# Half rows of the adjacency matrix loaded with a cast instead of copied first, and the first support product run beside the turning of h

## The chip, the cores and the metric

The kernel runs on one core of a Trainium2 chip. The core has a matrix engine (TensorE, PE in the profile, with its weight loads shown apart as PEld), a vector engine (VectorE, DVE), an activation engine (ScalarE, ACT), a general engine (GpSimd, POOL) and a queue engine that does nothing but issue transfers (SyncE, SP). Each works through its own instructions in order, and they wait for each other on counters called semaphores. Transfers run on 16 DMA engines that all queues share. Transfers of this kernel that change the data type are all issued from POOL, the others from SP or ACT.

The metric is device time in microseconds of one execution; lower is better.

## The reference, cut to what matters

Four graph layers run over N = 2708 nodes (padded to 2816 = 22 blocks of 128) with 256 features and a sparse 0/1 adjacency matrix `adj`. Each layer is `x = x + layer(relu(layernorm(x)), adj)`. Layer 0 is graph attention with 4 heads. Layer 1 is the one that the change is about:

```
node_adj_norm = adj with a zero diagonal
node_support  = node_adj_norm @ h                      # "support"
edge_output   = gru_cell(node_support, h, edge weights)
per head: hW = h @ W;  e = leaky_relu((node_adj_norm @ hW) @ a)
          att = softmax(where(node_adj_norm > 0, e, -9e15), axis=1);  out = (att * node_adj_norm) @ hW
node_output   = gru_cell(mean of the 3 heads, h, node weights)
result        = diag * edge_output + diag * node_output
```

The softmax needs, for each row and head, the largest `e` among the row's neighbours. Layer 2 is a neighbour mean with a linear map, layer 3 a distance-weighted sum that the kernel skips at run time when a check over all of `adj` finds nothing to add.

## The kernel before

The transposed adjacency matrix is kept in SBUF as fp8 (`AT`, 22 rows of blocks), loaded by POOL with a cast (lines 666 and 686). The instruction order of each engine is written out by hand; nothing is reordered later. The stages, in order of time:

- **Layer 0** (about 93 to 394 us). For 8 units (2 halves of the columns by 4 heads) and 22 row blocks, ACT makes a threshold (line 811), DVE two masks (lines 1130, 1136), and PE multiplies them with moving tiles 65 columns wide (line 1619), 44 weight loads and matmuls per step. Rings of 6 thresholds and 12 masks lie between the engines. Beside this, POOL loads the second half of `AT` (line 686) and then, in 22 transfers (line 689), copies `adj` from fp32 in HBM to `AH_D`, a bf16 copy in HBM; each waits for four more masks (`masks_built`). SP zeroes the diagonal of that copy.
- **Turning of h** (about 402 to 427 us). Per block t: ACT normalises (line 770), POOL casts the high fp16 part (697), DVE makes the low part (1224), PE transposes (1636), ACT or DVE evicts `HTS`, and PE multiplies it with a narrow matrix (1647).
- **Scores** (to about 471 us). PE multiplies `AT` with a 10 column matrix (line 1654, 484 matmuls), DVE works the scores out in steps, and they are written out and read back spread over all partitions (`EB`). In DVE's gaps PE runs the first support product, `support(0, c)`, cut in pieces (line 1665). `support(s, c)` covers blocks 2s and 2s+1 of the result and half c of the features: 44 matmuls, 256 columns wide, into PSUM bank c.
- **Edge steps** (about 471 to 708 us), t = 0 to 21. In a step PE runs one support product ahead, the head products (1677, 1679) and the GRU's products (1710, 1717). DVE takes its share of 88 "row maxima" (`row_max`, line 1316): each reads one half row block of `adj`, 128 x 1408 in bf16 (`AROW`, two buffers), against the scores of one head. Row L of the buffers serves heads 0 and 1, so 2 maxima per load. `rows_before(t)` says how many maxima are done when step t begins: 0, 5, 9, 14, 18, 22, 27, ... DVE's order in a step is: first maximum, `gru_blend` of the step before, the middle maxima, `support_low`, `products_low`, the last maximum, `gru_new`. POOL's part is `delta(t)` (line 703), which waits for ACT's tanh after `gru_new(t)` and is waited for by `gru_blend(t)`, and `apply` (708, 709). SP loads the half rows from `AH_D` (`load_row`, line 487); row L waits until both maxima of row L-2 are done, since it takes their buffer.
- **Attention** (about 710 to 1050 us). 9 units of 22 steps on PE (lines 1760, 1761), with the 44 maxima of the third head spread over the first 104 steps on DVE.
- Then the node GRU with layer 2's linear part, layer 2's sum and the output.

Of the kernel before, what the change touches and what calls it, by code (L numbers as in the profile page):

```python
# [18 lines left out]
def gnn_stack_kernel(nc, t_in, out):  # L19
# [60 lines left out]
    with ExitStack() as ctx:  # L80
# [78 lines left out]
        ZB = a0.take(NT, dt=BF16, size=2)  # L159
# [9 lines left out]
        assert NREAL <= (P - 1) * NT  # L169
# [96 lines left out]
        NOTI = sb("NOTI", [P, P])  # L266
# [17 lines left out]
        AH_D = nc.dram_tensor("adj_rows_half", [NT, P, N], BF16, kind="Internal").ap()  # L284
# [71 lines left out]

        def loads_before(t):

            return max(2, -(-rows_before(t) // 2))
# [52 lines left out]
        def _(sp):  # L412
# [49 lines left out]
            def load_halves(to, k, name):  # L462
                sp.dma_start(to, WS_D[k]).then_inc(sem(name), 16)

            sp.wait_ge(sem("rows_h"), 16 * NT)
            sp.dma_start(AH_D.rearrange("t p n -> (t p n)")[0:(P - 1) * NT * (N + 1)]
                         .rearrange("(a b c) -> a b c", b=NT, c=N + 1)[:, :, 0:1],
                         ZB[0:P - 1, :].unsqueeze(2), allow_slow_non_contiguous=True).then_inc(sem("rows_z"), 16)
            sp.wait_ge(sem("rows_z"), 16)
# [13 lines left out]
            def load_row(L):  # L483
                t, c = half_of(L)
                if L >= 2:
                    sp.wait_ge(sem("rmax"), maxima_after(L - 2))
                sp.dma_start(AROW[:, L % 2, :], AH_D[t, :, c * QUARTER:(c + 1) * QUARTER]
                             ).then_inc(sem(f"arow{L % 2}"), 16)

# [9 lines left out]
            for L in range(2):  # L499
                load_row(L)  # L500
# [37 lines left out]
            for t in range(NT):  # L538
                if t + 2 < NT:
                    load_h(t + 2, HR, 0)  # L540
                for L in range(loads_before(t + 1) if t else 2, loads_before(t + 2)):
                    load_row(L)
# [14 lines left out]
            for L in range(2 * NT, 2 * NT + 2):  # L557
                load_row(L)
# [12 lines left out]
            for m in range(len(units1) * NT):  # L571
                n, j = divmod(m, NT)
                h, g = units1[n]
                if m in row_at and row_at[m] + 2 < 4 * NT:
                    load_row(row_at[m] + 2)
# [68 lines left out]
        def _(pool):  # L644
# [10 lines left out]
            link(pool.memset(ZB, 0.0))  # L655
# [31 lines left out]
            for t in range(NT):  # L687
                pool.wait_ge(sem("masks_built"), 68 + 4 * t)
                pool.dma_start(AH_D[t], t_in["adj"][t * P:(t + 1) * P, :]).then_inc(sem("rows_h"), 16)

# [20 lines left out]
            for t in range(NT + 1):  # L711
                if t < NT:
                    delta(t, 0, HR, GT)
# [1239 lines left out]
```

## Time and profile before

| | us |
|---|---|
| median of 3 runs | 1334.71 (1331.9 to 1335.75) |
| profiled execution | 1334.99 |
| its span in the profile | 1332.9 |
| PE busy | 1140.3 |
| DVE busy | 937.4 |
| ACT busy | 785.0 |
| POOL busy | 216.7 |

The profile is of one execution. Its page gives busy time by engine, the chain of work that ended last, groups of instructions by line and the transfers. "issue" as a releaser is time in which an engine waited for nothing that the profile shows. PEclk is the clock granted to PE, as a share of 2.4 GHz: 1.00 is 2.4 GHz and 0.50 is 1.2 GHz. Busy shares are averages over stages with different limits, so what follows reads each stage by itself.

### The profile page before, as it was taken

What the parts mean: (1) busy time and instruction counts of PE and PEld (TensorE: products, weight loads), DVE (VectorE), ACT (ScalarE), POOL (GpSimd) and SP (SyncE); (2) the same over time, 40 slices, a digit from 0 to 9 for tenths busy, and PEclk for the clock granted to TensorE, in tenths of its full rate; (3) what the DMA queues carried; (4) which work ended last, traced back from release to release, by engine and by line L of the source; (5) the groups of instructions that cost most, each with busy time, mean ns of one, the idle gap of its engine ahead of it and who ended that gap; (6) DMA issues with size and microseconds to landing.
All of it is one profiled execution on the core that took longest, in us unless ns stands there. A gap on an engine that the chain in (4) does not pass through costs nothing.

```text
span 1332.9 us, 35106 instructions
## 1 busy us (share of the span) xinstructions
PE 1140.3 (86%) x15054; PEld 938.5 (70%) x15054; DVE 937.4 (70%) x2037; ACT 785.0 (59%) x1001; POOL 216.7 (16%) x296
## 2 busy tenths in 40 slices
PE   5529897987886989899978999999999997778997
PEld 4429887887885767666656888888888654446886
DVE  5786677767896289999995998769995365553541
ACT  3479988777735123332226999989989465653000
POOL 5631010000003012222222000001220141220000
PEclk9759999999995789999999999999999998899999
DMA  9936565556307343434336345417852010020532
GB/s 216 180 51 67 62 95 115 98 111 128 63 4 267 94 128 100 126 104 129 104 114 210 106 147 180 135 59 286 281 193 104 5 30 16 16 95 1 180 125 86
DMA packets 83731, 153.68 MB, mean 115 GB/s; under 512 B 9537, under 2 KB 60337, under 8 KB 82609
## 3 DMA queue, kind: packets, MB, share of 16 engines
q1 hardware_dynamic: 74993, 127.05, 30.8%
q0 software_dynamic: 7392, 23.79, 12.9%
q8 instruction: 120, 1.97, 0.6%
q10 hardware_dynamic: 1184, 0.53, 0.1%
q14 instruction: 42, 0.34, 0.1%
HBM read 171.26 MB, written 35.60 MB: 155 GB/s over the span
## 4 chain that ended last, share of the span: by engine, by line
PE 56%; DVE 23%; issue 8%; ACT 6%; DMA 3%; POOL 3%; ACTq 0%; SPq 0%; DVEq 0%; POOLq 0%
PE PS L1619 18%; PE PS L1760 10%; PE PS L1761 10%; DVE scratch L1316 9%; PE PS L1814 8%; PE PS L1710 3%; POOL arena L703 2%; PE PS L1801 2%; DVE arena L1298 2%; DVE arena L1090 2%; PE PS L1717 1%; PE PS L1587 1%; DMA arena<-e_rows 1%; DVE arena L1342 1%; PE PS L1654 1%
## 5 line engine op out<-in xcount | busy, mean ns | idle before, releaser
L1760 PE MATMUL PS<-arena 128*128 128x257 f16 x1452 | 325.5, 272 | 7.6 <-ACT arena L897 4.4
L1619 PE MATMUL PS<-arena 128*128 128x65 f16 x7744 | 259.1, 196 | 80.8 <-issue 41.3
L1761 PE MATMUL PS<-arena 128*128 128x257 f16 x1452 | 325.5, 274 | 0.0
L1619 PEld LDWEIGHTS PS<-arena 128*128 128x128 fp8e4 x7744 | 256.4, 99 | 83.4 <-issue 81.6
L811 ACT ACTIVATE arena<-arena 128x1408 fp8e4<-128x1408 f32 x176 | 242.5, 1456 | 51.4 <-DVE arena L1130 51.1
L1316 DVE CUSTOM_DVE_ANT_0 scratch<-arena 128x1408 bf16<-128x1408 bf16 x132 | 223.2, 1691 | 23.7 <-DMA arena<-e_rows 11.1
L897 ACT ACTIVATE arena<-arena 128x896 int16<-128x896 uint8 (+1 forms) x198 | 187.3, 973 | 22.8 <-DVE arena L1371 14.7
L1760 PEld LDWEIGHTS PS<-arena 128*128 128x128 bf16 x1452 | 142.7, 98 | 32.6 <-issue 8.6
L1761 PEld LDWEIGHTS PS<-arena 128*128 128x128 bf16 x1452 | 139.9, 96 | 21.5
L1130 DVE TENSOR_TENSOR arena<-arena,AT 128x352 int32<-128x352 int32 x176 | 91.3, 519 | 83.4 <-PE PS L1619 63.3
L888 ACT ACTIVATE arena<-arena,E1B 128x896 uint8<-128x896 f32 (+1 forms) x131 | 139.3, 1064 | 2.0 <-DMA arena<-m_rows 2.0
L876 ACT ACTIVATE arena<-arena 128x256 f32<-128x256 f32 x44 | 18.3, 417 | 186.1 <-DVE arena L1342 186.1
L1710 PE MATMUL PS<-arena 128*128 128x512 f16 x528 | 122.3, 382 | 0.4 <-ACT PS L860 0.4
L1665 PE MATMUL PS<-AT,arena 128*128 128x256 fp8e4 x968 | 111.5, 275 | 0.0
L703 POOL TENSOR_TENSOR arena<-arena 128x256 f32<-128x256 f32 x44 | 47.4, 1076 | 377.8 <-ACT arena L876 377.8
L1814 PE MATMUL PS<-arena,AT 128*128 128x256 f16 x968 | 106.2, 273 | 0.8 <-DVE X L1466 0.8
L1665 PEld LDWEIGHTS PS<-AT,arena 128*128 128x128 f16 x968 | 95.6, 99 | 12.1
L1814 PEld LDWEIGHTS PS<-arena,AT 128*128 128x128 fp8e4 x968 | 94.6, 98 | 12.5 <-DVE X L1466 1.1
L1371 DVE TENSOR_TENSOR arena<-arena,AT 128x224 int32<-128x224 int32 (+1 forms) x198 | 80.1, 432 | 19.2 <-ACT arena L888 19.0
L1710 PEld LDWEIGHTS PS<-arena 128*128 128x128 f16 x528 | 51.8, 98 | 56.8 <-issue 2.7
L1136 DVE TENSOR_TENSOR arena<-arena,AT 128x352 int32<-128x352 int32 x176 | 90.8, 516 | 0.0
L1423 DVE SCALAR_TENSOR_TENSOR scratch<-arena 128x1408 fp8e4<-128x1408 f32 x44 | 73.2, 1664 | 0.8 <-DMA arena<-in_adj 0.8
(189 smaller groups left out, 1333.3 us busy)
## 6 DMA issues: line engine op xcount, KB each, us to landing
arena<-adj_rows_half SPq DMA_DIRECT2D x88, 352.0 KB, 3.1
arena<-in_adj SPq DMA_DIRECT2D x44, 704.0 KB, 5.3
adj_rows_half<-in_adj POOLq DMA_DIRECT2D x22, 704.0 KB, 8.3
hw_saved<-arena SPq DMA_DIRECT2D x22, 387.0 KB, 4.3
AT<-in_adjT POOLq DMA_DIRECT2D x44, 176.0 KB, 8.0
arena<-hw_saved SPq DMA_DIRECT2D x9, 774.0 KB, 5.8
arena<-el_rows SPq DMA_DIRECT2D x8, 704.0 KB, 11.5
arena<-h_saved SPq DMA_DIRECT2D x44, 128.0 KB, 2.1
```

Of the source, the lines that this page charges most:

```text
L811: act.activation(THR[:, m % NTHR, :], ELB[:, n % 2, :], ACT.Sigmoid, bias=ERB[:, j, h:h + 1], scale=SHARP, saturate=False).then_inc(sem("t ...
L888: act.activation(Y[:, m % NRING, 0:nb * P], MB[n % 2][:, 0:nb * P], ACT.Relu, bias=E1B[:, j * H1 + h:j * H1 + h + 1], saturate=False).then ...
L897: act.activation(PWb[:, m % NRING, 0:nb * P], Y[:, m % NRING, 0:nb * P], ACT.Copy, scale=256.0).then_inc(sem("p_ready"), 1)
L1130: dve.tensor_tensor(mask_words(m, 0), THRi[:, m % NTHR, :], adj_words(m), ALU.bitwise_and).then_inc(sem("m_plus"), 1)
L1136: dve.tensor_tensor(mask_words(m, 1), mask_words(m, 0), adj_words(m), ALU.bitwise_xor).then_inc(sem("masks_built"), 1)
L1316: dve.tensor_tensor_reduce(junk, AROW[:, L % 2, :], eb[:, c * QUARTER:(c + 1) * QUARTER], 1.0, 0.0, ALU.mult, ALU.max, M2[:, c, h * NT + t ...
L1619: ins = pe.matmul(PS[:, first_bank(n) + i, (2 * r + q) * C0:(2 * r + q + 1) * C0], MASK[:, (m + j) % NMASK, q, k * P:(k + 1) * P], MOV[:, ...
L1665: ins = pe.matmul(PS[:, c, 0:D], HHL[:, j, a, c * P:(c + 1) * P], AT[:, j, i0 * P:i1 * P], start=(j == 0 and a == 0), stop=(j == NT - 1 an ...
L1710: ins = pe.matmul(PS[:, bank, :], half(c, a), w[:, c, b, 0:2 * D], start=False, stop=(w is wih and c == DC - 1 and a == 1), skip_group_che ...
L1760: pe.matmul(PS[:, k, 0:D + 1], weights, w[:, 0:D + 1], start=(j == 0), stop=False)
L1761: ins = pe.matmul(PS[:, k, 0:D + 1], weights, w[:, D + 2:2 * D + 3], start=False, stop=(j == NT - 1))
L1814: ins = pe.matmul(o, AT[:, j, t * P:(t + 1) * P], YHL[:, j, a, :], start=(j == 0 and a == 0), stop=(j == NT - 1 and a == 1))
```

## The change

Three things are changed.

1. The bf16 copy of `adj` in HBM goes, with its 22 transfers, the zeroing of its diagonal and the waits of SP for both. `load_row` moves from SP's queue to POOL's and reads `adj` itself in fp32, casting to bf16 on the way. DVE zeroes the diagonal block in SBUF ahead of the first maximum that uses it (heads 0 and 2).
2. In POOL's loop over the edge steps, loads stand at three places: ahead of `delta(t)`, behind it, and behind `apply(t - 1)`.
3. PE runs `support(0, c)` one block at a time beside the turning of h, and `support(1, c)` in the gaps of the scores where `support(0, c)` was. Steps 0 and 1 then have no support product. ACT's and DVE's evictions of the first product move forward with it.

```diff
+            def load_row(L):
+                t, c = half_of(L)
+                if L >= 2:
+                    pool.wait_ge(sem("rmax"), maxima_after(L - 2))
+                pool.dma_start(AROW[:, L % 2, :], t_in["adj"][t * P:(t + 1) * P, c * QUARTER:(c + 1) * QUARTER]
+                               ).then_inc(sem(f"arow{L % 2}"), 16)
+            load_row(0)
+            load_row(1)
+            fetched = 2
...
             for t in range(NT + 1):
+                while t < NT and 2 * fetched < rows_before(t + 1):
+                    load_row(fetched)
+                    fetched += 1
                 if t < NT:
                     delta(t, 0, HR, GT)
+                while fetched < 2 * NT + 2 and maxima_after(fetched - 2) <= min(rows_before(t + 1) + 1, rows_before(t + 2)):
+                    load_row(fetched)
+                    fetched += 1
                 if t >= 1:
                     apply(t - 1, 0, HR)
+                while fetched < 2 * NT + 2 and maxima_after(fetched - 2) <= min(rows_before(t + 1) + 2, rows_before(t + 2)):
+                    load_row(fetched)
+                    fetched += 1
             pool.wait_ge(sem("hw_mm"), NT)
             for m in range(len(units1) * NT):
+                if m in row_at and row_at[m] + 2 < 4 * NT:
+                    load_row(row_at[m] + 2)
...
-                pool.dma_start(AH_D[t], t_in["adj"][t * P:(t + 1) * P, :]).then_inc(sem("rows_h"), 16)
...
+                if h != 1 and c == diagonal_half(t):
+                    at = t * P - c * QUARTER
+                    block = AROW[:, L % 2, at:at + P].bitcast(mybir.dt.int32)
+                    link(dve.tensor_tensor(block, block, NOTI[:].bitcast(mybir.dt.int32), ALU.bitwise_and))
                 dve.tensor_tensor_reduce(junk, AROW[:, L % 2, :], ...
...
             for t in range(NT):
                 if t + 1 < NT:
                     l1_transposes(t + 1)
...
+                support(0, 0, t, t + 1)
+                support(0, 1, t, t + 1)
...
-            support(0, 0, 0, 11)
+            support(1, 0, 0, 11)
...
-                if s + 1 < len(SUP):
+                if 2 <= s + 1 < len(SUP):
                     support(s + 1, c)
```

How this stands on POOL's queue in the first edge steps. Before (L703 is `delta`, L708 and L709 are `apply`):

```order
43 L703 TENSOR_TENSOR arena<-arena 128x256 [waits n,hr0]
44 L703 TENSOR_TENSOR arena<-arena 128x256 [waits n,hr1]
45 L708 TENSOR_SCALAR arena<-arena,DN 128x256 [waits blend]
46 L709 TENSOR_TENSOR X<-X,arena 128x256 [waits pool_chain]
47 L703 TENSOR_TENSOR arena<-arena 128x256 [waits n,hr2]
```

And after, from `delta(0)` to `delta(3)` (L673 is `load_row`, L684 `delta`, L689 and L690 `apply`):

```order
43 L684 TENSOR_TENSOR arena<-arena 128x256 [waits n,hr0]
44 L673 DMA arena<-in_adj 128x1408 [waits rmax] x2
45 L684 TENSOR_TENSOR arena<-arena 128x256 [waits n,hr1]
46 L673 DMA arena<-in_adj 128x1408 [waits rmax] x2
47 L689 TENSOR_SCALAR arena<-arena,DN 128x256 [waits blend]
48 L690 TENSOR_TENSOR X<-X,arena 128x256 [waits pool_chain]
49 L684 TENSOR_TENSOR arena<-arena 128x256 [waits n,hr2]
50 L673 DMA arena<-in_adj 128x1408 [waits rmax] x2
51 L689 TENSOR_SCALAR arena<-arena,DN 128x256 [waits blend]
52 L690 TENSOR_TENSOR X<-X,arena 128x256 [waits pool_chain]
53 L673 DMA arena<-in_adj 128x1408 [waits rmax]
54 L684 TENSOR_TENSOR arena<-arena 128x256 [waits n,hr3]
```

The loads that stood on SP's queue now stand behind `delta`, in pairs or singly; the two of row 44 are L = 3 and 4, those of row 46 are L = 5 and 6, those of row 50 are L = 7 and 8, and row 53 is L = 9.

On PE at the beginning of the turning of h, before (L1636 transposes, L1647 is the narrow product):

```order
390 L1636 MATMUL PS<-identh,arena 128x128 [waits lo1]
391 L1636 MATMUL PS<-identh,arena 128x128 x3
392 L1647 MATMUL PS<-U1S,arena 128x3 [waits hts_dve]
393 L1647 MATMUL PS<-U1S,arena 128x3 x5
394 L1636 MATMUL PS<-identh,arena 128x128 [waits hts_dve,lo1]
```

After (L1632 transposes, L1656 is the narrow product, L1643 is `support`):

```order
390 L1632 MATMUL PS<-identh,arena 128x128 [waits lo1,diag0]
391 L1632 MATMUL PS<-identh,arena 128x128 x3
392 L1656 MATMUL PS<-U1S,arena 128x3 [waits hts_dve]
393 L1656 MATMUL PS<-U1S,arena 128x3 x5
394 L1643 MATMUL PS<-AT,arena 128x256 x4
395 L1632 MATMUL PS<-identh,arena 128x128 [waits hts_dve,lo1]
```

Four matmuls 256 columns wide are added per block, 88 in all, between the narrow product of one block and the transposes of the next but one.

## Rows read from the trace of the kernel before

**Rows 1.** The page: busy time by engine, and the chain that ended last.
```profile
PE 1140.3 (86%) x15054; PEld 938.5 (70%) x15054; DVE 937.4 (70%) x2037; ACT 785.0 (59%) x1001; POOL 216.7 (16%) x296
...
PE 56%; DVE 23%; issue 8%; ACT 6%; DMA 3%; POOL 3%; ACTq 0%; SPq 0%; DVEq 0%; POOLq 0%
```

**Rows 2.** Stretches, whole core: length, busy (instructions) by engine, clock, DMA share, GB/s.
```profile
95.00:190.00 95.00, 86.02 (x2566) 85.31 (x2564) 67.62 (x146) 87.04 (x65) 10.77 (x21) 0.95 0.57 62
190.00:355.00 165.00, 132.91 (x3961) 131.08 (x3958) 117.28 (x266) 128.79 (x95) 12.12 (x23) 0.97 0.60 115
355.00:394.00 39.00, 38.29 (x1193) 38.16 (x1192) 33.51 (x82) 19.72 (x17) 0.00 (x0) 1.00 0.11 5
```

**Rows 3.** Waits, 190:355: waiter, releaser, us, times, longest.
```profile
PE PS L1619 <- issue: 30.9, 16, 3.6
```

**Rows 4.** Chain of waits, 186:356: start us, us, what.
```profile
by line: PE PS L1619 80.3%; issue 19.8%
...
229.17 3.58 issue
232.75 5.70 PE PS L1619 x128
```

**Rows 5.** The page's DMA issues: KB written each, median us to landing.
```profile
arena<-adj_rows_half SPq DMA_DIRECT2D x88, 352.0 KB, 3.1
arena<-in_adj SPq DMA_DIRECT2D x44, 704.0 KB, 5.3
```

**Rows 6.** Line 686, casting load of adjT: us from issue to landing.
```profile
DMA to landing us min/median/max: 4.1/4.4/8.7
```

**Rows 7.** Line 689, casting copy of adj: us from issue to landing.
```profile
DMA to landing us min/median/max: 6.3/8.3/12.5
```

**Rows 8.** Line 487, half-row load of before: us from issue to landing.
```profile
DMA to landing us min/median/max: 2.8/3.1/9.0
```

**Rows 9.** Timeline, DVE, 524.5:537.5: start us, us, instruction, [idle before].
```profile
524.92 1.62 DVE L1316 CUSTOM_DVE_ANT_0 scratch<-arena 128x1408 bf16<-128x1408 bf16 x1
...
527.16 0.43 DVE L1349 SCALAR_TENSOR_TENSOR arena<-arena 128x256 f32<-128x256 f32 x1 [0.61 <-POOL arena L703]
...
528.04 2.14 DVE L1316 CUSTOM_DVE_ANT_0 scratch<-arena 128x1408 bf16<-128x1408 bf16 x1
...
530.37 1.63 DVE L1316 CUSTOM_DVE_ANT_0 scratch<-arena 128x1408 bf16<-128x1408 bf16 x1 [0.17 <-DVE M L1316]
```

**Rows 10.** Timeline, POOL, same stretch.
```profile
525.59 1.53 POOL L703 TENSOR_TENSOR arena<-arena 128x256 f32<-128x256 f32 x1 [7.80 <-ACT arena L876]
```

**Rows 11.** Line 703, POOL's difference, both layers.
```profile
L703 POOL TENSOR_TENSOR arena<-arena x44: 724/728/1697, 480.7 to 1191.3; 128x256 f32<-128x256 f32 x44
```

**Rows 12.** Lines 1371 and 1211, DVE's masking of int32 words.
```profile
L1371 DVE TENSOR_TENSOR arena<-arena,AT x198: 371/389/1821, 711.6 to 1032.2; 128x224 int32<-128x224 int32 x132, 128x256 int32<-128x256 int32 x66
...
L1211 DVE TENSOR_TENSOR AT<-AT,arena x1: 184/184/184, 389.3 to 389.3; 128x32 int32<-128x32 int32 x1
```

**Rows 13.** Timeline, PE, 405:458.
```profile
406.15 1.01 PE L1636 MATMUL PS<-identh,arena 128*128 128x128 f16 x8 [12.63 <-DVE arena L1224]
...
429.06 6.56 PE L1654 MATMUL PS<-arena,AT 128*128 128x10 f16 x240 [1.67 <-DVEq L1244]
...
444.37 4.49 PE L1665 MATMUL PS<-AT,arena 128*128 128x256 fp8e4 x22
...
449.45 2.57 PE L1665 MATMUL PS<-AT,arena 128*128 128x256 fp8e4 x22
```

**Rows 14.** Stretches, as rows 2.
```profile
402.00:427.00 25.00, 15.97 (x214) 13.04 (x214) 16.29 (x47) 15.74 (x31) 10.86 (x23) 0.50 0.77 251
...
470.00:700.00 230.00, 208.18 (x1513) 147.62 (x1512) 211.12 (x354) 66.75 (x152) 56.10 (x55) 0.98 0.39 112
```

**Rows 15.** Timeline, DVE, line 1316 in 729:850, first and last of 36.
```profile
729.83 1.62 DVE L1316 CUSTOM_DVE_ANT_0 scratch<-arena 128x1408 bf16<-128x1408 bf16 x1 [5.28 <-issue]
...
849.75 1.62 DVE L1316 CUSTOM_DVE_ANT_0 scratch<-arena 128x1408 bf16<-128x1408 bf16 x1
```

More of the change, by code:

```diff
@@ L540, in _ @@
                     load_h(t + 2, HR, 0)
-                for L in range(loads_before(t + 1) if t else 2, loads_before(t + 2)):
-                    load_row(L)
                 if t == NT - 2:
@@ L556, in _ @@
                         load_products(0, c)
-            for L in range(2 * NT, 2 * NT + 2):
-                load_row(L)
             for i in range(2):
@@ L847, in support_high @@
                 act.activation(NSH[:, s % 2, c, 0, :], PS[:, c, 0:D], ACT.Copy).then_inc(sem("ns_hi"), 1)
+            for c in range(DC):
+                support_high(0, c)
+            act.wait_ge(sem("fr_arg"), 1)
+            act.activation(FR, FR, ACT.Exp).then_inc(sem("fr"), 1)
             def products_high(t):
@@ L908, in _ @@
             gate_bias_n(1, 0, BIAS)
-            for c in range(DC):
-                support_high(0, c)
             act.wait_ge(sem("frw"), 1)
@@ L1245, in _, with support_low @@
             bias_sum(BIAS, BRB, "be", "bias_e")
+            def support_low(s, c):
+                dve.wait_ge(sem("ns_hi"), DC * s + c + 1)
+                dve.tensor_tensor(NSH[:, s % 2, c, 1, :], PS[:, c, 0:D], NSH[:, s % 2, c, 0, :],
+                                  ALU.subtract).then_inc(sem("ns_lo"), 1)
+            for c in range(DC):
+                support_low(0, c)
             dve.wait_ge(sem("dn"), 16)
@@ L1372, in mask @@
                                   ).then_inc(sem("y_masked"), 1)
-            for c in range(DC):
-                support_low(0, c)
             for t in range(NT + 1):
@@ L1668, in support @@
                     ins.then_inc(sem("ns"), 1)
+            l1_transposes(0)
+            pe.wait_ge(sem("diag0"), DIAG0)
+            for t in range(NT):
+                if t + 1 < NT:
+                    l1_transposes(t + 1)
+                pe.wait_ge(sem("hts_dve" if t % 2 == 0 else "hts_act"), t // 2 + 1)
+                for c in range(DC):
+                    for a, b in TERMS:
+                        ins = pe.matmul(PS[:, 5, t * H1:(t + 1) * H1], HTS[:, t, (DC * a + c) * P:(DC * a + c + 1) * P],
+                                        U1S[:, c, b, 0:H1], start=(c == 0 and a + b == 0), stop=(c == DC - 1 and a == 1))
+                ins.then_inc(sem("hu_mm"), 1)
+                support(0, 0, t, t + 1)
+                support(0, 1, t, t + 1)
+            pe.wait_ge(sem("up"), 1)
+            for t in range(NT):
+                for j in range(NT):
+                    ins = pe.matmul(PS[:, 4, t * 10:(t + 1) * 10], AT[:, j, t * P:(t + 1) * P], UP[:, j, :],
+                                    start=(j == 0), stop=(j == NT - 1))
+            ins.then_inc(sem("e_mm"), 1)
             def products(t):
```

54 lines of the change are left out of this document (4 added, 50 removed).

## The prediction, made before the changed kernel was run

> **What bounds the kernel now.** I read the page first [rows 1]: PE is busy 86% of the span and DVE 70%, and the chain of waits lies 56% on PE and 23% on DVE. So no single engine bounds the whole, and each stage has to be read by itself. The change touches four: layer 0, the turning of h, the edge steps and the attention.
>
> Layer 0, by the table of stretches and the waits. From 190 to 355 us PE issues 3961 matmuls in 165 us, 41.7 ns each; from 355 to 394 us it issues 1193 in 38.29 us of busy time, 32.1 ns each [rows 2]. The first stretch holds the 22 transfers of line 689 and the second has almost no traffic (DMA share 0.60 against 0.11). In the first PE stands 30.9 us idle in 16 gaps put down to "issue" [rows 3], 19.8% of that stretch's chain [rows 4]. Each gap ends a run of 128 matmuls or a multiple: 128 weight loads and 128 matmuls, 256 instructions. After a gap of 3.58 us the next 128 take 5.70 us [rows 4] instead of the 4.1 that 32.1 ns make. I read this as PE waiting for its instructions, which come over the same DMA engines.
>
> Edge steps, by the stretches and the timelines of DVE and POOL. DVE is busy 211.12 of 230 us [rows 14], so it is the bound, with PE close behind it. The first maximum of a step (524.92) is followed by a wait for POOL's `delta` (525.59 to 527.12), then the blend (527.16), the second maximum (528.04, stretched to 2.14 us while POOL works) and the third (530.37) [rows 9, 10]. No line of DVE's there waits for a half row: those land 3.1 us after their issue [rows 8].
>
> **The change part by part.**
>
> *Copy of adj removed.* If PE ran at 32.1 ns, the 3961 matmuls would take 127.1 us, 37.9 less than 165. If it ran as from 95 to 190 us, where casting loads of `adjT` share the DMA engines (2566 in 95 us, 37.0 ns), they would take 146.6, 18.4 less [rows 2]. The score loads of SP stay in the stretch. I take the idle time of the waits itself, 30.9: **-31** (from -38 to -18). ACT can follow: its 95 thresholds from 190 to 355 use 128.79 us, 1.36 each, and a step of 44 matmuls at 32.1 ns takes 1.41.
>
> The Trainium skill ("Runtime: NRT & Kernel Launch", Instruction fetch mechanics) says that instructions are fetched in blocks of 256 by a DMA queue of the sequencer and that crossing a block is mostly hidden. The trace agrees on the 256 and not on the hiding. By the rule alone this term would be near 0, which is the third rival.
>
> *Half rows on POOL's queue.* The price is the wait of a maximum for its row. How long the new load takes is not in the trace. The nearest row is line 686: the same 128 x 1408 fp32 elements read with a cast on the same queue, 4.1 / 4.4 / 8.7 us [rows 6]. It writes 176 KB, the new one 352 KB. The fp32 loads of SP write 704 KB and take 5.3 us [rows 5]; the cast of twice the source takes at least 6.3 [rows 7]; the half row of before, half the bytes read, 2.8 to 3.1 [rows 8]. I take T = 4.4, near the row of the same source, with 4.1 to 5.3 as bounds and 2.8 and 6.3 as far ends.
>
> Where the loads stand decides the rest. Let a be the first maximum of a step. The order shows the first load behind `delta(t)`, though its buffer was free earlier, so it is issued at 527.12 on the clock of the step in [rows 9, 10] and lands at 527.12 + T. Three kinds of step follow from `rows_before`:
> - a even and its own row already there (a = 18, 22, 40, 44, ...): the load behind `delta` is for maximum a+2, needed at 530.37. Stall T - 3.25 = 1.15. In steps 1 to 19 there are 7.
> - a odd (5, 9, 27, 31, ...): the load is for a+1, needed at 528.04. Stall T - 0.92, less 0.52 since that maximum no longer runs beside POOL (1.62 for 2.14): 2.96. There are 8.
> - a even, with maximum a of a row not yet asked for (14, 36, 58, 80): DVE stands at its first instruction. `delta` runs without DVE beside it, in 0.73 us [rows 11], so the load goes at 526.32 and the maximum starts at 530.72, not 524.92. The blend comes at 532.34, not 527.16, and the 0.52 comes back: 4.66. There are 4.
>
> Together 7 x 1.15 + 8 x 2.96 + 4 x 4.66 = **+50.4**. With T = 4.1 it is 44.7, with 5.3 67.5, with 3.1 26.7, with 2.8 23.1, with 6.3 86.5. Nothing hides it, since DVE is the bound. PE's idle time grows with it, and the GRU's products are ready several us before `gru_new` asks for them, so that PE stays off the path. The other loads of a step are issued as soon as their buffer is free and have 5 us or more.
>
> The Trainium skill ("DMA: Bandwidth & Descriptors", Anatomy of one DMA, SWDGE path) gives a fit for loads from POOL, 2.0 us plus the bytes over 436 GB/s: 3.65 us for the 720,896 bytes read, below every casting load of line 686. By it the three kinds would cost an estimated 36 us instead of 50, and the forecast would be 14 lower. The measured row decides.
>
> *Zeroing the diagonal in SBUF.* 22 of the 44 rows of heads 0 and 1 carry a diagonal block, so 22 more DVE instructions of 128 x 64 words and a wait on each. 128 x 32 words take 0.184 us and 128 x 224 take 0.389 [rows 12], so 64 take 0.22; with half of the 0.17 us that a maximum waits for the one before [rows 9] it is 0.3 each: **+6.6** (22 x 0.184 = 4 up to 22 x (0.389 + 0.17) = 12). The row itself must have landed, so the stalls don't hide them. 22 more in the attention are in the next term.
>
> *Third head's rows.* 36 maxima start from 729.83 to 849.75 [rows 15], 3.43 us apart. From the end of one to the start of the next but one there are 2 x 3.43 - 1.7 = 5.15 us, less 0.3 for a mask: enough for T = 4.4 on average, not for the closest ones. DVE has slack there and rings of 6 tiles lie before PE. **+2** (0 to 10; 10 is T = 5.3, 0.45 us short in each of 22 pairs).
>
> *Support beside the turning.* PE starts at 406.15 and has nearly all of the 22 blocks done at 427, at a clock of 0.50 [rows 13, 14]: it is busy 15.97 us, 0.73 per block, and one block comes every 0.95 us. Four support matmuls take 0.8 us at that clock (22 in 4.49) and 0.44 at full (22 in 2.57) [rows 13]. The same product, once started at 444.37, brought the clock from 1.2 to 2.4 GHz within its first 22 matmuls. If it does so here, three blocks run at 1.53 us and the rest at about 0.37 + 0.44 = 0.8, below the 0.95 at which they come: the 1.7 us lost are made up within some 12 blocks. **0** (0 to +13). Support 1 fills the gaps of the scores as support 0 did, and is as long. The 2 x 44 matmuls that leave steps 0 and 1 (10 us) were run while DVE waited for its scores or worked off its maxima, so they give **0** as well. SP's shorter queue gives 0: DVE waited for none of it.
>
> The sum on the profiled execution: 1334.99 - 31 + 50.4 + 6.6 + 2 = 1363.0 us. That execution lies 0.3 us above the median of the runs shown, so it stands for the median. Some of the rows may land later than 4.4 us where the product stores share the engines; I leave that to the range.
>
> **The rivals.**
> - *The casting load is as quick as the half row was (the other side).* It needs T of 2.8 to 3.1 [rows 8]. With 2.8, layer 0 at its full rate and masks at 4: 1335 - 37.9 + 23.1 + 4 = 1324; with 3.1 and my other terms: 1335 - 31 + 26.7 + 6.6 = 1337. It decides once stalls and masks cost less than the 31 to 38 of layer 0. For it: its bytes written are those of the half row. Against: all 22 casts of line 686 took 4.1 or more for half the bytes written.
> - *Loads of 5.3 us and more, and the attention runs short too.* 1335 - 31 + 67.5 + 6.6 + 10 = 1388. For it: the fp32 loads take this, and the store of the head products falls close by.
> - *The gaps of layer 0 stay,* since score loads or the queue itself cause them: 1363 + 31 = 1394. Against it: from 355 us on there is no such gap.
> - *PE's clock stays at 1.2 GHz in the turning.* 22 blocks of 1.53 us from 406.15 end at 439.8 instead of 427: 1363 + 13 = 1376. For it: the narrow matmuls from 429.06 to 444.4 did not raise it [rows 13].
>
> **How the numbers follow.** The forecast gets 0.55, with its own range 1345 to 1385; the quick load 0.14, the slow load 0.15, the gaps that stay 0.08, the clock that stays 0.08. 1363 is the likeliest. The range of 8 in 10 goes from 1338, above most of the quick load's times, to 1398, just past the gaps that stay. Faster or slower by 0.3% (4 us) is what a measurement of this kernel tells from no change. Of the quick load's 0.14 I give 0.09 to faster and 0.04 to same; all else is slower: 0.87.
>
> **What would show it.** In the edge steps DVE's maxima wait for a transfer from `adj` in 19 steps, in three sizes near 1.2, 3.4 and 6 us, with a mean step of about 14.4 us instead of 11.5 (230 us over 20 steps). From 190 to 355 us PE's waits for "issue" fall to a few us and layer 0 ends near 363 us instead of 394. The clock of the turning rises within its first 5 us, and the narrow matmuls start within 1 us of where they stood, counted from the start of the turning. New int32 operations of 0.2 to 0.3 us stand before 22 maxima. The prediction is wrong if the first wait behind `delta` is under 2 us where a is odd, if layer 0 ends later than 375 us, or if PE waits in the attention for DVE's masks by more than 10 us.

## The result, and the profile after

The changed kernel takes 1365.12 us (median of 4 runs, 1363.87 to 1366.34). The kernel before takes 1335.23 on the same chip. The ratio is 1.0224 with a 95% interval of 1.0196 to 1.0252. The forecast of 1363.0 was 2 us off, and the sign was right. The table has the marks of the profiled executions, in us from the span's start. Each was read off the timeline: the last matmul 65 columns wide, the first transpose of h, the first `delta`, the first matmul 257 columns wide, and the first identity matmul 512 columns wide behind them.

| | before | after | after - before |
|---|---|---|---|
| layer 0 ends | 393.5 | 353.75 | -39.8 |
| turning of h starts | 406.15 | 367.52 | -38.6 |
| `delta(0)` | 480.69 | 442.55 | -38.1 |
| edge stage, `delta(0)` to attention | 233.9 | 289.0 | +55.1 |
| attention | 334.0 | 346.1 | +12.0 |
| the rest, to the span's end | 284.3 | 282.8 | -1.5 |
| span | 1332.9 | 1360.4 | +27.5 |

The span grew by 27.5 us and the profiled execution by 28.9 (1334.99 to 1363.87), so 1.4 us of the change lie outside the span.

The page first, busy time by engine and the chain that ended last, as [rows 1]:

```profile
PE 1146.9 (84%) x15054; PEld 934.6 (69%) x15054; DVE 943.2 (69%) x2081; ACT 783.8 (58%) x1001; POOL 247.7 (18%) x361
...
PE 48%; DVE 22%; DMA 12%; issue 8%; ACT 5%; POOL 4%; DVEq 0%; SPq 0%; POOLq 0%; ACTq 0%
```

DMA holds 12% of the chain where it held 3%. Layer 0 is answered by the stretches, as [rows 2], and by PE's wait for "issue" from 190 to 355 us, as [rows 3]:

```profile
95.00:190.00 95.00, 87.48 (x2629) 87.24 (x2627) 67.92 (x146) 87.24 (x65) 14.73 (x21) 0.95 0.57 64
190.00:355.00 165.00, 162.18 (x5074) 161.71 (x5070) 147.72 (x345) 145.35 (x110) 0.24 (x1) 1.00 0.07 18
```
```profile
PE PS L1615 <- issue: 1.3, 2, 0.7
```

The first stretch is nearly as before. In the second PE issues 5074 matmuls where it issued 3961, and the 30.9 us of gaps have become 1.3. Behind it comes the turning, PE's timeline, as [rows 13]:

```profile
367.52 1.01 PE L1632 MATMUL PS<-identh,arena 128*128 128x128 f16 x8 [13.77 <-DVE arena L1216]
368.62 0.32 PE L1656 MATMUL PS<-U1S,arena 128*128 128x3 f16 x6
368.81 1.01 PE L1643 MATMUL PS<-AT,arena 128*128 128x256 fp8e4 x4
...
373.12 0.72 PE L1643 MATMUL PS<-AT,arena 128*128 128x256 fp8e4 x4
...
374.06 0.60 PE L1643 MATMUL PS<-AT,arena 128*128 128x256 fp8e4 x4
...
390.12 4.19 PE L1664 MATMUL PS<-arena,AT 128*128 128x10 f16 x152 [1.22 <-DVEq L1236]
397.11 3.58 PE L1664 MATMUL PS<-arena,AT 128*128 128x10 f16 x128 [2.80 <-issue]
402.24 5.67 PE L1664 MATMUL PS<-arena,AT 128*128 128x10 f16 x204 [1.55 <-issue]
```

Four support matmuls take 1.01 us in the first three blocks, then 0.72 and 0.60: the clock rose from its lower to its upper level 5.6 us after the start of the turning, with PE at work without a break from that start on. The narrow matmuls begin 22.6 us after that start (22.9 before). Two gaps of 2.80 and 1.55 us now lie among them. The clock does not stay up for them. The stretches, as [rows 2], one ahead of the narrow matmuls and one over the first 152 of them:

```profile
375.00:390.00 15.00, 13.80 (x227) 11.53 (x223) 9.98 (x28) 12.57 (x25) 8.28 (x16) 1.00 0.80 221
390.12:394.31 4.19, 4.19 (x152) 4.10 (x152) 2.05 (x4) 0.56 (x1) 0.00 (x0) 0.54 1.07 284
```

The granted clock is 1.00 in the first and 0.54 in the second, so it fell back within the first microsecond of the narrow matmuls.

Edge steps: DVE's timeline has the three kinds of stall (one of each here), POOL's has the loads behind `delta`, as [rows 9, 10].

```profile
462.49 1.63 DVE L1314 CUSTOM_DVE_ANT_0 scratch<-arena 128x1408 bf16<-128x1408 bf16 x1 [3.40 <-DMA arena<-in_adj]
...
477.54 1.63 DVE L1314 CUSTOM_DVE_ANT_0 scratch<-arena 128x1408 bf16<-128x1408 bf16 x1 [5.67 <-DMA arena<-in_adj]
...
506.05 0.22 DVE L1313 TENSOR_TENSOR arena<-arena,NOTI 128x64 int32<-128x64 int32 x1 [0.85 <-DMA arena<-in_adj]
```
```profile
456.65 1.52 POOL L684 TENSOR_TENSOR arena<-arena 128x256 f32<-128x256 f32 x1 [11.52 <-ACT arena L870]
458.12 1.10 POOL L673 DMA_DIRECT2D arena<-in_adj  x2
...
472.45 0.72 POOL L684 TENSOR_TENSOR arena<-arena 128x256 f32<-128x256 f32 x1 [11.86 <-ACT arena L870]
473.12 1.14 POOL L673 DMA_DIRECT2D arena<-in_adj  x2
```

(The timeline merges instructions that follow each other, so x2 is a pair of loads.) At 458.12 the loads go out right behind `delta(1)`, and the maximum that needs the first of them starts at 462.49, 4.37 us later. Read through to the end of the stage, the timeline has 19 such waits, in three sizes: 8 of 3.08 to 3.46 (26.4 in all), 7 of 0.69 to 1.80 (7.0), 4 of 5.65 to 5.90 (23.1). Their sum is in DVE's waits, 442 to 732 us (us in total, times, longest):

```profile
DVE scratch L1314 <- DMA arena<-in_adj: 28.6, 9, 5.9
DVE arena L1313 <- DMA arena<-in_adj: 27.8, 10, 5.8
```

Line 1313 is the new zeroing of the diagonal block. The casting load (line 673, us to landing) and the zeroing by themselves, as [rows 6] and [rows 12]:

```profile
DMA to landing us min/median/max: 4.1/4.4/8.3
```
```profile
L1313 DVE TENSOR_TENSOR arena<-arena,NOTI x44: 211/224/226, 427.6 to 914.2; 128x64 int32<-128x64 int32 x44
```

Attention, 731 to 1078 us, DVE's waits for rows and PE's wait for DVE:

```profile
DVE arena L1313 <- DMA arena<-in_adj: 15.5, 11, 4.3
...
DVE scratch L1314 <- DMA arena<-in_adj: 8.4, 8, 4.1
```
```profile
PE PS L1758 <- DVE arena L1408: 9.2, 3, 5.0
```

DVE waits 23.9 us for rows. PE waits 9.2 us for line 1408, DVE's eviction of a finished unit, which stands in DVE's queue behind a maximum that waits. The same eviction cost PE 0.9 us before. Each of its two long waits costs more than its own length, since the clock is at its lower level behind it. PE's timeline at the first, and the stretches with the first and the second, as [rows 2]:

```profile
779.54 0.36 PE L1758 MATMUL PS<-arena 128*128 128x257 f16 x1 [5.03 <-DVE arena L1408]
```
```profile
771.52:791.52 20.00, 14.97 (x120) 12.26 (x119) 16.42 (x39) 14.21 (x17) 2.31 (x4) 0.91 0.57 101
851.52:871.52 20.00, 16.54 (x136) 13.94 (x137) 18.48 (x43) 16.67 (x18) 2.94 (x5) 0.91 0.63 126
```

Ahead of the wait of 5.03 us the matmuls 257 columns wide start 0.11 us apart. The first 16 behind it start 0.22 us apart, and so do the first 14 behind the other one, of 3.83 us. That makes an estimated 1.7 and 1.5 us, most of the 3.5 us by which PE is busier in this attention with the same work (331.6 us, and 328.1 before). The 12.0 us by which the attention grew are 8.6 us more of idle time and 3.5 us of slower matmuls.

### The profile page after: what moved, and what is told of

Read it like the earlier page. It is cut to its first block, busy times and chain, and to the rows that moved or that the text cites. A ratio compares the mean times of both kernels' runs of the same rounds, so it can differ in the third digit from the quotient of the medians.

```text
span 1360.4 us, 35125 instructions
## 1 busy us (share of the span) xinstructions
PE 1146.9 (84%) x15054; PEld 934.6 (69%) x15054; DVE 943.2 (69%) x2081; ACT 783.8 (58%) x1001; POOL 247.7 (18%) x361
## 4 chain that ended last, share of the span: by engine, by line
PE 48%; DVE 22%; DMA 12%; issue 8%; ACT 5%; POOL 4%; DVEq 0%; SPq 0%; POOLq 0%; ACTq 0%
PE PS L1615 16%; DMA arena<-in_adj 10%; PE PS L1812 8%; DVE scratch L1314 7%; PE PS L1758 7%; PE PS L1759 7%; PE PS L1708 3%; PE PS L1799 2%; POOL arena L684 2%; DVE arena L1292 2%; DVE arena L1082 2%; PE PS L1643 1%; PE PS L1715 1%; DMA arena<-e_rows 1%; PE PS L1664 1%
## 5 line engine op out<-in xcount | busy, mean ns | idle before, releaser
L1615 PE MATMUL PS<-arena 128*128 128x65 f16 x7744 | 252.4, 195 | 49.8 <-DVE arena L1128 40.9
L1615 PEld LDWEIGHTS PS<-arena 128*128 128x128 fp8e4 x7744 | 251.7, 98 | 50.4 <-issue 50.1
L803 ACT ACTIVATE arena<-arena 128x1408 fp8e4<-128x1408 f32 x176 | 240.4, 1456 | 15.8 <-DVE arena L1122 15.8
L1314 DVE CUSTOM_DVE_ANT_0 scratch<-arena 128x1408 bf16<-128x1408 bf16 x132 | 217.7, 1649 | 44.6 <-DMA arena<-in_adj 37.0
L891 ACT ACTIVATE arena<-arena 128x896 int16<-128x896 uint8 (+1 forms) x198 | 187.0, 972 | 34.3 <-DVE arena L1369 26.4
L1708 PE MATMUL PS<-arena 128*128 128x512 f16 x528 | 126.8, 392 | 0.6 <-ACT PS L854 0.6
L1675 PE MATMUL PS<-arena 128*128 128x512 f16 x132 | 58.9, 474 | 67.9 <-DVE arena L1292 67.9
L1643 PE MATMUL PS<-AT,arena 128*128 128x256 fp8e4 x968 | 115.7, 277 | 0.0
L684 POOL TENSOR_TENSOR arena<-arena 128x256 f32<-128x256 f32 x44 | 44.5, 1012 | 328.9 <-ACT arena L870 328.9
L1643 PEld LDWEIGHTS PS<-AT,arena 128*128 128x128 f16 x968 | 94.0, 99 | 11.7
L673 POOL DMA_DIRECT2D arena<-in_adj x88 | 50.9, 579 | 233.2 <-DVE M L1314 233.2
```

What stands on the lines that cost most here:

```text
L803: act.activation(THR[:, m % NTHR, :], ELB[:, n % 2, :], ACT.Sigmoid, bias=ERB[:, j, h:h + 1], scale=SHARP, saturate=False).then_inc(sem("t ...
L891: act.activation(PWb[:, m % NRING, 0:nb * P], Y[:, m % NRING, 0:nb * P], ACT.Copy, scale=256.0).then_inc(sem("p_ready"), 1)
L1314: dve.tensor_tensor_reduce(junk, AROW[:, L % 2, :], eb[:, c * QUARTER:(c + 1) * QUARTER], 1.0, 0.0, ALU.mult, ALU.max, M2[:, c, h * NT + t ...
L1615: ins = pe.matmul(PS[:, first_bank(n) + i, (2 * r + q) * C0:(2 * r + q + 1) * C0], MASK[:, (m + j) % NMASK, q, k * P:(k + 1) * P], MOV[:, ...
L1643: ins = pe.matmul(PS[:, c, 0:D], HHL[:, j, a, c * P:(c + 1) * P], AT[:, j, i0 * P:i1 * P], start=(j == 0 and a == 0), stop=(j == NT - 1 an ...
L1708: ins = pe.matmul(PS[:, bank, :], half(c, a), w[:, c, b, 0:2 * D], start=False, stop=(w is wih and c == DC - 1 and a == 1), skip_group_che ...
```

## The experiments

All times are medians. Ratios are to the kernel before, run beside them on the same chip. Marks are of one profiled execution each, and the changed kernel and the seven kernels with an identical layer 0 end it up to 5.5 us apart (351.7 to 357.15 us), so I compare stages by their lengths.

### Loads asked for ahead of `delta`: e1_loads_ahead

```diff
-                while t < NT and 2 * fetched < rows_before(t + 1):
+                while t < NT and fetched < 2 * NT + 2 and maxima_after(fetched - 2) <= rows_before(t + 1):
```

> The changed kernel with one condition of POOL's loop changed: ahead of delta(t) it issues every half row whose buffer is free once the maxima of step t are done, instead of only the rows that step t itself needs. Loads, bytes, masks and everything else stay. Theory (the stalls of the edge steps come from where the loads stand, behind delta): the row for maximum a+1 or a+2 is issued when its buffer comes free, 4 to 8 us before it is needed, so nearly all of the 56 us that DVE waits for rows in the edge steps go; the stage gets about 50 us shorter and the kernel comes to about 1315. Rival (two buffers and 4.4 us of landing are the limit, wherever the loads stand): DVE still waits 20 us or more there, and the time is above 1340.

Measured: 1317.98 us, 0.9864 (0.9816 to 0.9912). The edge stage is 240.4 us instead of 289.0. DVE's waits in it:

```profile
DVE arena L1347 <- POOL arena L684: 14.3, 21, 1.4
DVE scratch L1314 <- DVE M L1314: 3.1, 18, 0.2
...
DVE arena L1313 <- DMA arena<-in_adj: 0.2, 1, 0.2
```

The same loads, as many and equally long (4.1 / 4.4 / 8.4 us to landing), on the same queue: only their place differs. 56.4 us of waits for rows have become 0.2, and 48.6 us of the stage are gone. So the stalls came from where the loads stand, and not from the cast. The attention is unchanged (346.3).

### Copy back in layer 0, whole, in halves and in quarters: e2_copy_back, e4_copy_halves, e7_copy_quarters, b1_before_halves

The first three are the changed kernel with the 22 casting copies put back (nobody reads the copy). The last is the kernel before with its copies cut in two.

```diff
+            for t in range(NT):
+                pool.wait_ge(sem("masks_built"), 68 + 4 * t)
+                pool.dma_start(AH_D[t], t_in["adj"][t * P:(t + 1) * P, :]).then_inc(sem("rows_h"), 16)
...
+                for c in range(2):   # e4, b1: two pieces; e7: four of half that width
+                    pool.dma_start(AH_D[t, :, c * QUARTER:(c + 1) * QUARTER], ...
```

> The changed kernel with the 22 transfers that copy adj to a bf16 copy in HBM issued again in layer 0, from POOL as in the kernel before; nothing reads the copy. Theory (these transfers hold up PE's instructions): layer 0 ends near 393 us instead of 354, PE's idle time put down to issue from 190 to 355 us is back at about 31 us, and the time is 1365 + 38 = 1403. Rival (layer 0 got shorter for another reason, such as the order of POOL's queue): layer 0 ends below 365 and the time stays under 1375.

Measured: 1412.22 us, 1.0574 (1.0521 to 1.0626). The turning starts at 408.13 us instead of 367.52. The stretch from 190 to 355 us, and PE's wait in it:

```profile
190.00:355.00 165.00, 132.09 (x3870) 130.48 (x3868) 113.85 (x259) 122.89 (x90) 11.73 (x22) 0.94 0.55 110
```
```profile
PE PS L1620 <- issue: 32.9, 15, 5.3
```

The gaps are back, with nobody reading the copy, so they belong to these transfers. The matmuls between them take 34.1 ns each (132.09 over 3870). The time is 9 us above the 1403 that was expected: the turning starts 40.6 us late instead of 38, and the attention is 350.1 us long instead of 346.1.

> As e2_copy_back, but each of the 22 transfers is issued as two, 128 rows of 1408 columns each, instead of whole rows: the same bytes over the same queue in 44 transfers of smaller pieces (2816 B written each instead of 22,528). Theory A (it is the length of the pieces: an instruction fetch has to wait for the piece that a DMA engine is in): the gaps shrink, layer 0 ends between 354 and 370, and the time is 1365 to 1380. Theory B (it is the volume or the queue's load): the gaps are as in e2_copy_back and the time is about 1403.

Measured: 1397.87 us, 1.0475 (1.0418 to 1.0531). The same wait:

```profile
PE PS L1622 <- issue: 22.8, 16, 5.0
```

> e2_copy_back with each of the 22 transfers issued as four, 128 rows of 704 columns each (1408 B written per piece, the size that the casting loads of adjT write). Same bytes, 88 transfers. Halves gave PE 22.8 us of issue idle from 190 to 355 us instead of 32.9 and 14 us less time. If the length of the pieces sets the gaps, quarters bring them to 10 to 15 us and the time to 1380 to 1388. If it is the bytes, with halves only spread better, they stay at 20 to 24 us and the time at 1394 to 1402.

Measured: 1402.16 us, 1.0494 (1.0449 to 1.0539).

```profile
PE PS L1623 <- issue: 22.2, 13, 5.5
```

> The kernel before with its 22 copies of adj issued as two halves of 1408 columns each, nothing else changed. If the gaps of layer 0 depend on the pieces as e4_copy_halves against e2_copy_back showed (14 us), this kernel takes about 1321; if that difference belonged to the changed kernel's later stages, it stays at 1334.

Measured: 1330.16 us (11 runs), 0.995 (0.9926 to 0.9974), the turning starting at 395.63 instead of 406.15.

```profile
PE PS L1621 <- issue: 23.2, 16, 4.4
```

What follows: smaller pieces help once. Halves take 8 to 10 us off the gaps (32.9 to 22.8, and 30.9 to 23.2 in the kernel before), quarters nothing more that can be told (the intervals of the two overlap), and the longest gap stays at 4.4 to 5.5 us. e4 and b1 fell between the times that their two theories gave, e7 came out by its second. Against the changed kernel the turning starts 40.6 us late with whole copies, 24.9 with halves (392.46) and 28.9 with quarters (396.39). So over 60% of the price stays however the transfers are cut; cutting them is half a remedy. b1's profile is of its fastest run, 8.3 us below its median, so the 10.5 us that it gains by the turning flatter the halves; the ratio of 0.995 is about 7 us.

That PE waits for its instructions in these gaps can be read from the transfers themselves. The page's queue q8, kind "instruction", carries 120 transfers of 16,384 bytes in the kernel before. From 190 to 355 us there are 31 of them for 3961 matmuls and as many weight loads, one for every 256 instructions. Each of the 16 gaps there ends 2.2 to 2.5 us after one of these transfers begins. So do the gaps of e2, e4 and b1. The transfer is not longer beside the copies (median 0.97 us, and 1.04 without them). It comes too late, and what delays its start stays open.

### First support product back where it was: e3_support_back, e9_early_support_back

```diff
-                support(0, 0, t, t + 1)
-                support(0, 1, t, t + 1)
...
-            support(1, 0, 0, 11)
+            support(0, 0, 0, 11)
...
-                if 2 <= s + 1 < len(SUP):
+                if s + 1 < len(SUP):
```

> The changed kernel with its third part undone: support 0 runs in the gaps of the scores again and support 1 in steps 0 and 1. Theory (the moved product was hidden before and is hidden after, worth nothing): 1365 within 3 us, the narrow matmuls starting within 1 us of the same distance from the start of the turning. Rival (the move was worth something, since PE's clock is up when the narrow matmuls begin and 10 us of PE work leave the first steps): 1370 or more, 5 to 10 us slower than the changed kernel.

Measured: 1369.6 us, 1.0254 (1.0203 to 1.0305). From the end of layer 0 to `delta(0)` it takes 87.6 us (after: 88.8), and the edge stage 289.8 (289.0). The attention is 350.0 us instead of 346.1, with the same instructions. The time lies between what the theory and the rival gave. The difference in the attention settles nothing: of the kernels with two row buffers for the third head, e2 and e4 keep the third part of the change and have 350.1 and 350.4 us as well. So I repeated the pair on a kernel without these waits (e8, below).

> e8_rows_early with the third part of the change undone: support(0, c) in the gaps of the scores, support(1, c) in step 0, as in the kernel before. My theory: that part costs and gives nothing, so this is within 3 us of e8_rows_early; up to the attention it is 1 to 2 us earlier, since the score matmuls follow 2 us sooner, and the attention is equally long. Rival 1 (the part costs what the 2.4 us longer score stage shows): 2 to 4 us faster than e8_rows_early. Rival 2 (it gives something, as the attention of e3_support_back, 3.9 us longer, might be read): 3 us or more slower.

Measured: 1313.02 us, 0.9833 (0.9816 to 0.9849), against 1312.06, 0.9825 (0.9807 to 0.9842). From the end of layer 0 to `delta(0)` 88.5 us against 88.7, edge stage 246.7 against 246.5, attention 334.4 against 334.1. The third part of the change neither costs nor gives anything that can be seen here. The longer score stage of the early product (17.3 us against 15.8 of narrow matmuls) is caught up before `delta(0)`.

### Zeroing left out: e6_no_masks

e1_loads_ahead without the zeroing of the diagonal:

```diff
-                if h != 1 and c == diagonal_half(t):
-                    at = t * P - c * QUARTER
-                    block = AROW[:, L % 2, at:at + P].bitcast(mybir.dt.int32)
-                    link(dve.tensor_tensor(block, block, NOTI[:].bitcast(mybir.dt.int32), ALU.bitwise_and))
```

> e1_loads_ahead without the 44 instructions that zero the diagonal block in SBUF; the maxima of heads 0 and 2 then see the diagonal, which is left out of the computation otherwise. Theory (each costs about 0.3 us of the edge steps, where DVE is the bound): the edge steps take 234 us instead of 240.4 and the time is about 1311 to 1312. Rival (the 6.5 us left of the edge steps are late rows, not masks): the edge steps stay above 238 and the time within 2 us of 1318.

Measured: 1307.89 us, 0.9794 (0.975 to 0.9839). The edge stage is 235.7 us instead of 240.4, so the 22 operations in it cost 4.7 us, 0.21 each, which is no more than their own 0.224. 1.8 us over the 233.9 of before stay unexplained. Outside the span this kernel has 1.9 us, as the kernel before (2.1), where e1_loads_ahead has 3.4: the zeroing costs 1.5 us there too, in what way no run shows. The profile is of the fastest run, 5.9 us below the median. The attention is 343.5 instead of 346.3, and DVE still waits for its rows there:

```profile
DVE scratch L1310 <- DMA arena<-in_adj: 25.0, 23, 4.0
```

### Six row buffers for the third head, and when to fill them: e5, e8, e10

Once heads 0 and 1 are done, the score rows of head 1 are free, and hold four more half rows. All three kernels build on e1_loads_ahead.

```diff
+        AROW3 = arena[:, rows_at + N:rows_at + 2 * N].bitcast(BF16).rearrange("p (a b) -> p a b", a=4)
...
+                if L >= 2 * NT + 6:
+                    pool.wait_ge(sem("rmax"), maxima_after(L - 6))
+                elif L >= 2 * NT + 2:
+                    pool.wait_ge(sem("rmax"), PAIRED)        # e10: PAIRED + 1
...
+            for L in range(2 * NT + 2, 2 * NT + 6):          # e8: in the edge loop, behind apply(18)
+                load_row(L)
             for m in range(len(units1) * NT):
-                if m in row_at and row_at[m] + 2 < 4 * NT:
-                    load_row(row_at[m] + 2)
+                if m in row_at and row_at[m] + 6 < 4 * NT:
+                    load_row(row_at[m] + 6)
```

> e1_loads_ahead with six buffers instead of two for the third head's half rows in the attention: the four more lie where the scores of head 1 were, which nothing reads by then. Rows, masks and loads are the same in number. Theory (the attention is 12 us longer than before because a row of two buffers cannot land in time for maxima close together, so that DVE comes late to the evictions that PE waits for): the 23 us that DVE waits for rows there go, PE's waits for the evictions fall from 9 us to about 1, the attention is back at 334 to 337 us from 346, and the kernel comes to about 1307. Rival (it is the masks, or the heavier transfers of fp32 rows slowing PE's instructions): the attention stays at 343 us or more and the time above 1314.

Measured: 1315.55 us, 0.9841 (0.979 to 0.9891). DVE's waits for rows are gone, and its eviction makes PE wait 0.6 us. But the attention is 343.8 us, only 2.5 shorter. The timelines of POOL, SP, DVE and PE at its start show why:

```profile
693.25 2.32 POOL L691 DMA_DIRECT2D arena<-in_adj  x4
```
```profile
693.34 0.37 SPq L487 DMA_DIRECT2D arena<-e_rows  x1
```
```profile
710.00 0.23 DVE L1333 TENSOR_TENSOR arena<-arena,NOTI 128x64 int32<-128x64 int32 x1 [13.16 <-issue]
```
```profile
714.04 0.39 PE L1778 MATMUL PS<-arena 128*128 128x257 f16 x1 [7.93 <-ACT arena L911]
```

The four rows and the scores of the third head are issued in the same moment. The scores take 16.6 us to land, the longest of that line's three loads; the maximum that waits for them starts 16.7 us after their issue, where 8.5 us lay between the two in e1_loads_ahead:

```profile
DMA to landing us min/median/max: 7.2/11.7/16.6
```

DVE stands for 13.16 us at a maximum that waits for them, its masks are queued behind, and PE runs dry. The numbers came out as the rival had them (343 or more, above 1314), but neither the masks nor slower instructions are the reason, as the next two kernels show.

> e5_six_buffers with its four extra rows of the third head asked for three edge steps before the end, while POOL has nothing else to do, instead of just ahead of the attention. In e5_six_buffers the four loads were issued at 693.25 us and the scores of the third head (the load of e_rows) at 693.34; those scores took 16.6 us to land where they took 8.5 in e1_loads_ahead, DVE's first maximum of the third head started at 710.0, and PE stood up to 7.9 us for the masks that DVE had not reached. Theory (the four loads crowd out the load of the scores): the scores land in about 8.5 us again, PE's wait of 7.9 goes, the attention comes from 343.8 down to 336 us (334.0 of the kernel before and 22 masks on DVE), and the time is 1315.6 - 8 = 1307.5. Rival (the wait has nothing to do with the loads, for instance the scores are written late): the attention stays near 344 and the time near 1315.

Measured: 1312.06 us, 0.9825 (0.9807 to 0.9842). The maximum that waits for the scores starts 7.6 us after their issue, and the attention is 334.1 us, as long as before. But the edge stage has grown from 240.4 to 246.5. SP's timeline, and PE's at the start of the attention:

```profile
672.76 0.31 SPq L518 DMA_DIRECT2D m_rows<-ET  x1
678.98 0.33 SPq L527 DMA_DIRECT2D arena<-m_rows  x1
```
```profile
689.27 0.38 PE L1779 MATMUL PS<-arena 128*128 128x257 f16 x1 [9.25 <-ACT arena L912]
```

The four row loads were issued at 671.28 us. The small store of `m_rows` behind them took 6.2 us until the load that waits for it could go (1.4 in e5), and the first masks of the attention wait for that load. The wait was moved, not removed, and the time is 4.6 us above the 1307.5 expected.

> e5_six_buffers with its four extra rows of the third head asked for once the first maximum of that head is done, so behind the load of the scores (e_rows) and behind the small transfers of m_rows ahead of the attention. In e8_rows_early the four loads stood beside the write of m_rows: 6.2 us lay between it and the load that waits for it where there were 1.4, and PE stood 9.2 us before the last step of the edge stage; its attention itself was 334.1 us long, as in the kernel before. Theory (any small transfer on which a stage waits is held up by four row loads issued at once): here nothing urgent is under way beside them. The edge stage is 240.2 us as in e1_loads_ahead and e5_six_buffers, the scores land in 8.5 us, the attention is 334 to 337 us long, the time is 1312 - 6 + 1 = 1307. Rival (masks and rows cost DVE something in the attention anyway, and e8's short attention came from its later start): the attention is 340 us or more, the time 1312 or more.

Measured: 1302.51 us (5 runs, 1302.13 to 1305.08), 0.9757 (0.972 to 0.9794). The edge stage is 240.3 us and the attention 335.1. It is the fastest of all, 2.4% under the kernel before, and 4.5 us below what was expected. Rows and masks are as many as in e1_loads_ahead, so the rival fails. PE's waits in its attention:

```profile
PE PS L1778 <- ACT arena L911: 6.0, 4, 2.5
...
PE PS L1778 <- DVE arena L1430: 0.8, 2, 0.5
PE PS L1778 <- DVE arena L1428: 0.6, 2, 0.3
```

## Why the prediction was right, and which terms were not

*Half rows on POOL's queue* (+50.4). Right in place, kind and size. T is 4.4 us as taken, with the same 4.1 at the low end as the row it was read from [rows 6]. The three kinds come 7, 8 and 4 times, as counted from `rows_before`. The waits were to be 1.15, 3.48 (2.96, and the 0.52 that the maximum gains by not running beside POOL) and 5.80 us (from 524.92 to 530.72). They are 1.00, 3.30 and 5.76 in the mean. e1 prices their removal at 48.6 us. The term rested on the order of POOL's queue and one landing time, both of which could be read before.

*Zeroing* (+6.6). e6 has 4.7 us in the edge stage. What I added for the wait on each operation did not show. Another 1.8 us of the stage are not explained, so the two together are 6.5. Where the term put nothing, outside the span, e6 shows 1.5 us more.

*Copy removed* (-31). This is the term of the sum that was mis-sized. It measured -38.6 by the start of the turning and -39.8 by the end of layer 0, at and beyond my end of -38. The step that failed is "I take the idle time of the waits itself". The same stretch held a second cost, matmuls that ran slower between the gaps: 132.91 us over 3961 are 33.6 ns each [rows 2], against 32.0 in the same stretch after (162.18 over 5074). That is 6.3 us more, and with the 29.6 of gaps that went it makes 35.9. The prediction showed the sign of it, the 5.70 us of the 128 matmuls behind a gap [rows 4], and read it as waiting for instructions. It was the clock: from 233.3 to 236.3 us the granted clock is 0.50 and 61 matmuls take 3.00 us, 49 ns each. Three runs of 128 behind gaps of 3.0 to 3.6 us take 5.70, 5.67 and 5.50 us where the others take 4.2, which is 4.2 of the 6.3 us. The remaining 3 to 4 us up to -39.8 are within the 5.5 us by which the end of layer 0 scatters. My upper end had the slower matmuls in, as the full rate, and the gaps that I expected to be left came to 1.3 us.

*Third head's rows* (+2, 0 to 10). Outside my range: +12.0. I said that DVE has slack and that rings lie before PE. The rings cover masks, but not the evictions, which stand in DVE's same queue and free PE's banks: PE waits 9.2 us for them instead of 0.9, and the clock, at its lower level behind the two long waits, costs most of the other 3.5. I also judged by the mean distance of the maxima, 3.43 us. Their real distances vary, and DVE waited 19 times, up to 4.3 us. e10 shows that buffers are what was missing: 335.1 us with six of them, masks included, and PE busy for 326.8 us at a granted clock of 1.00.

*Support beside the turning* (0). Right. The clock rose after three blocks and e9 finds no difference. Of my marks, the start of the narrow matmuls held (22.6 us for 22.9), and the clock rose 5.6 us after the start, a little later than the 5 that I gave. The two gaps among the narrow matmuls, 4.35 us together, were not in the working.

The two sizes that were off were of opposite sign, 8 to 9 us too little gained in layer 0 and 10 too little lost in the attention. That they nearly cancel, and the total is closer than these terms are, is luck. Of the marks given beforehand, layer 0 ended at 353.75, 9 us sooner than the 363 I named, for the reason above. The mean step, `delta(0)` at 442.55 to `delta(19)` at 717.32, was 14.46 us where 14.4 was named. I had put the point where the account would be wrong at 10 us of waits of PE for DVE's masks in the attention. PE waits 10.3 us for DVE there (9.2 and another 1.1), all of it for evictions; by its words the mark was not reached, but it named the wrong work.

Of the rivals, the quick load fails on 4.4 us, the slow one as well, though the short attention that it had with it came true (+12.0 for its +10) at 4.4 us. The gaps of layer 0 did not stay, and the clock did not stay low in the turning. The Trainium skill ("DMA: Bandwidth & Descriptors", Anatomy of one DMA, SWDGE path) gave 3.65 us for this load by its fit; the trace has 4.4, and 4.1 at the least, so the fit is low by 0.75 us here, and by it the three kinds would have been an estimated 14 us too small. What the Trainium skill ("Runtime: NRT & Kernel Launch", Instruction fetch mechanics) says, that crossing a block of instructions is mostly hidden, holds in this kernel's stretch without the copies (1.3 us of gaps in 165), and fails beside them (32.9 us in e2).

## What to carry to other kernels

A transfer that waits for a buffer belongs in its queue at the point where the buffer comes free, and not behind an instruction that waits for something else. The same loads cost the edge stage 48.6 us at one place of POOL's queue and at most the unexplained 1.8 at another. Where a row then must come in ahead of time, look at what small transfer is under way in the same moment, and which stage waits for it: four row loads of 720,896 bytes each, read with a cast, held up a load by 8 us and a store by 5, and cost nothing that shows once the load was in. And before a mean distance is taken for slack, look at what else stands in the waiting engine's queue; here it was the eviction, and not the masks, that reached PE. A wait of the matrix engine can also cost more than it lasts: behind those of 5.0 and 3.8 us some 15 matmuls each ran at the lower clock level, an estimated 1.5 to 1.7 us more (0.22 us from start to start instead of 0.11).

## What the runs showed of the hardware that was not expected

- Bulk copies from HBM to HBM with a cast held up PE's instructions more than their share of the DMA engines tells. The share was 0.60 beside the copies and 0.57 beside the casting loads ahead of them [rows 2]. PE lost 30.9 of 165 us to gaps there (19%) and 9.0 of 95 here (9%). The bytes moved do differ, 115 GB/s against 62 [rows 2], but with the copies cut in halves, at the same 115 GB/s, the gaps are 23.2 us (b1).
- Narrow matmuls of 10 columns hardly depend on the clock. The first 152 of them take 4.19 us in the changed kernel at a granted clock of 0.54, 27.6 ns each, and 4.03 us in e2 at 0.86, 26.5 ns each. At 0.50 in the kernel before they take 27.3 (240 in 6.56 us) [rows 13]. No run has a long stretch of them at 1.00.

```profile
430.61:434.64 4.03, 4.03 (x152) 3.94 (x152) 2.05 (x4) 0.56 (x1) 0.00 (x0) 0.86 1.08 257
```
